# Attention operands split in three parts: high parts in two buffers, rests and low parts on GpSimd, another order of loads and stores

## The reference, cut to what matters

```python
# token stage, for each of the 4 batches
scores = q @ k.T                        # 1024 x 1024
h = prelu((gamma * scores) @ v @ Wo + bo)
# attention stage: 8 heads of 8 features, 4 x 8 = 32 heads in all
xn = layernorm(h)
q, k, v = split(xn @ qkv_w + qkv_b)
h = h + softmax(q * scale @ k.T + bias) @ v @ proj_w + proj_b
# expert stage: layernorm twice, top 2 of 8 experts, weights from a softmax
h = h + sum_e w_e * (gelu(xn2 @ W1[e] + b1[e]) @ W2[e] + b2[e])
```

## Time and profile before

| | us |
|---|---|
| median of 3 runs | 549.04 |
| lowest, highest run | 546.72, 556.23 |
| the profiled execution | 548.42 |
| its span, first to last instruction | 546.5 |
| PE busy | 517.1 (95%) |
| DVE busy | 455.0 (83%) |
| ACT busy | 356.9 (65%) |
| POOL busy | 88.8 (16%) |

### The profile page before, as it was taken

How to read it: one execution, slowest core, us unless ns; L and a number is a source line. 1 busy time by engine, 2 the same in 40 slices (tenths; PEclk the granted TensorE clock), 3 DMA queues, 4 the chain that set the end, 5 groups by cost and what they waited for, 6 DMA issues and landing times.

```text
span 546.5 us, 12886 instructions
## 1 busy us (share of the span) xinstructions
PE 517.1 (95%) x4179; PEld 179.8 (33%) x4179; DVE 455.0 (83%) x538; ACT 356.9 (65%) x633; POOL 88.8 (16%) x186
## 2 busy tenths in 40 slices
PE   7998989698999999999999999999999989999996
PEld 5332333332333333333333333333333343233321
DVE  2679778778999999999999999999999787766644
ACT  2021122245898888898898988988988866455442
POOL 8702021233100100100100001001001360211000
PEclk9999999878999999999999999999999999999999
DMA  7600046983432332332322323323334100100000
GB/s 276 191 4 1 0 129 184 268 241 96 119 88 62 89 83 58 90 78 61 88 76 71 79 75 82 78 65 86 79 85 126 59 11 11 43 20 1 20 19 20
DMA packets 51096, 45.28 MB, mean 83 GB/s; under 512 B 26266, under 2 KB 39035, under 8 KB 51067
## 3 DMA queue, kind: packets, MB, share of 16 engines
q1 hardware_dynamic: 51066, 44.89, 29.6%
HBM read 28.70 MB, written 16.17 MB: 82 GB/s over the span
## 4 chain that ended last, share of the span: by engine, by line
PE 78%; DVE 8%; DMA 5%; issue 3%; SPq 3%; ACT 2%; POOL 1%; DVEq 0%; ACTq 0%; POOLq 0%
PE ps L1516 25%; PE ps L1407 14%; PE ps L1501 12%; PE ps L1677 6%; PE ps L1593 5%; PE ps L1324 3%; PE ps L1335 3%; DVE gated L972 2%; DVE nmax L951 1%; PE ps L1505 1%; PE ps L1421 1%; PE ps L1660 1%; DMA maxima<-max_t 1%; SPq L383 1%; DMA q_ring<-maxima 1%
## 5 line engine op out<-in xcount | busy, mean ns | idle before, releaser
L951 DVE TENSOR_REDUCE nmax<-ps 128x1 f32<-128x1024 f32 x256 | 301.8, 1218 | 19.8 <-PE ps L1407 11.1
L804 ACT ACTIVATE probs<-ps 128x512 f32<-128x512 f32 x512 | 278.1, 596 | 47.3 <-PE ps L1501 37.3
L1516 PE MATMUL ps<-probs,v_ring 128*32 128x256 f32 x2048 | 164.1, 393 | 0.0
L1501 PE MATMUL ps<-q_ring,k_ring 51*128 51x512 bf16 x512 | 100.4, 381 | 5.3 <-ACT probs L804 1.5
L1407 PE MATMUL ps<-k_ring,q_ring 48*128 48x512 bf16 x512 | 100.6, 389 | 2.3 <-DVE nmax L951 1.5
L1516 PEld LDWEIGHTS ps<-probs,v_ring 128*32 128x32 f32 x2048 | 40.5, 108 | 61.9 <-issue 36.9
L1407 PEld LDWEIGHTS ps<-k_ring,q_ring 48*128 48x128 bf16 x512 | 24.7, 93 | 107.5 <-issue 99.2
L1233 DVE TENSOR_TENSOR probs<-probs,ps 128x1024 f32<-128x1024 f32 (+1 forms) x33 | 39.1, 1187 | 25.1 <-PE ps L1660 19.6
L820 ACT ACTIVATE probs<-ps,wide_w 128x1024 f32<-128x1024 f32 x32 | 35.4, 1114 | 33.5 <-PE ps L1593 32.5
L972 DVE SCALAR_TENSOR_TENSOR gated<-ps,v_s,gamma_sb 128x1024 f32<-128x1024 f32 x32 | 40.3, 1278 | 14.9 <-PE ps L1324 13.6
L625 POOL TENSOR_TENSOR max_p<-nmax,zeros 128x8 bf16<-128x8 f32 x32 | 6.5, 202 | 274.7 <-DVE nmax L951 267.0
(11 more groups left out here) (173 smaller groups left out, 348.7 us busy)
## 6 DMA issues: line engine op xcount, KB each, us to landing
k_ring<-qk_parts SPq DMA_DIRECT2D x64, 96.0 KB, 2.4
q_ring<-qk_parts SPq DMA_DIRECT2D x64, 96.0 KB, 2.4
gamma_sb<-gamma_t SPq DMA_DIRECT2D x4, 1024.0 KB, 8.7
v_padded<-v_pad SPq DMA_DIRECT2D x4, 1024.0 KB, 6.1
v_ring<-v_padded SPq DMA_DIRECT2D x32, 128.0 KB, 3.2
outputs<-o_t SPq DMA_DIRECT2D x32, 128.0 KB
qk_parts<-qk_h SPq DMA_DIRECT2D x8, 384.0 KB, 4.7
x_ring<-bias_parts SPq DMA_DIRECT2D x32, 96.0 KB, 3.1
```

The lines of the kernel that those rows point to most:

```text
L804: A.activation(probs[:, s % 4, HALF * j:HALF * (j + 1)], ps[:, key_bank(s, j), :], ACT.Exp).then_inc(exp_done[j], 1)
L951: V.tensor_reduce(nmax[:, par, s:s + 1], ps[:, bank:bank + 2, :].rearrange("p a n -> p (a n)"), AX, ALU.max, negate=True).then_inc(s1_redu ...
L1501: last = mm(ps[:, key_bank(s, j), :], k_ring[rows, u, P * s:P * (s + 1)], q_ring[rows, u, HALF * j:HALF * (j + 1)], start=True, stop=not c ...
L1516: last = mm(ps[VC * j:VC * (j + 1), PVB, 0:2 * P], v_ring[:, u, m, :], probs[:, m % 4, 2 * P * j:2 * P * (j + 1)], start=(m == 0), stop=(m ...
```

## The change

What is computed stays the same; what moves is who splits the operands, and in which order. The steps:

1. `qk_h` has two buffers, used in turn. The high part of batch n waits for the store of batch n - 2 and for the rest of batch n - 2.
2. All rests and low parts are POOL's. DVE's `rest_part` and `low_part` are gone. ACT therefore keeps the float32 value of every batch, those of batches 0 and 1 in `qk_rest`; PE's `project_vv`, which overwrites the PSUM bank, now waits for that copy.
3. DVE's `norm_scale(0)` and `norm_scale(1)` stand behind the first gate of the next batch, where they stood behind the last gate of their own.
4. ACT squares for batches 1 and 2 ahead of the next copy out of PSUM or of the middle part; `square(3)` stands between the high part and the keep of batch 2.
5. POOL's `bias_residual`, which adds the projection's bias to h, stands ahead of `power` for batches 0 to 2.
6. SP loads the operands of heads 0 and 1 behind batch 0's stores, those of head 2 behind batch 1's and those of head 3 behind batch 2's stores of high, values and middle. Batch 1's values are stored between its high and its middle part. At the end, the maxima of head 0 go out ahead of batch 3's high part, and the rows come back ahead of batch 3's values.

The diff, cut to its core:

```diff
-        qk_h = sb("qk_h", [P, T], bf16)
+        qk_h = sb("qk_h", [P, 2, T], bf16)
...
-                sp.wait_ge(qk_h_ready, b + 1)
-                store_parts(b, 0, qk_h)
+                def store_high():
+                    sp.wait_ge(qk_h_ready, b + 1)
+                    store_parts(b, 0, qk_h[:, b % 2, :])
+
                 if b == B - 1:
-                    send_max_rows(0, 0, 0, store_values)
-                elif b >= LATE:
+                    send_max_rows(0, 0, 0, store_high)
+                else:
+                    store_high()
+                if b >= LATE:
+                    store_values()
+                if b == 1:
                     store_values()
                 sp.wait_ge(qk_m_ready, b + 1)
                 store_parts(b, 1, m_of(b))
+                if b == 0:
+                    store_values()
                 if b < LATE:
-                    store_values()
                     store_low(b)
...
-                    for u in range(RING):
+                    for u in range(2):
                         load_operands(u, u)
                         load_values(u, u)
+                elif b < RING - 1:
+                    load_operands(b + 1, b + 1)
+                    load_values(b + 1, b + 1)
...
-            for n in range(B):
+            for n in range(B - 1):
+                if n == B - 2:
+                    rest_part(n - 1)
+                bias_residual(n)
                 power(n)
-                if n < B - 1:
-                    bias_residual(n)
+                if n == B - 3:
+                    rest_part(n - 1)
+                if n >= 1:
+                    low_part(n - 1)
+            power(B - 1)
             rest_part(B - 2)
             split_maxima(0, 0)
             rest_part(B - 1)
...
             def high_part(n):
...
-                act.wait_ge(qk_stored[0], n * 2 * 16)
-                if n == B - 1:
-                    act.wait_ge(qk_r_ready, n)
-                A.activation(qk_h[:, :], flat(5, 7), ACT.Identity, bias=qk_bias[:, 0:1]).then_inc(qk_h_ready, 1)
+                if n >= 2:
+                    act.wait_ge(qk_stored[0], (n - 1) * 2 * 16)
+                    act.wait_ge(qk_r_ready, n - 1)
+                A.activation(qk_h[:, n % 2, :], flat(5, 7), ACT.Identity, bias=qk_bias[:, 0:1]).then_inc(qk_h_ready, 1)
...
                 if b >= 2:
                     leave_hn(b - 2)
+                if b == B - 1:
                     high_part(b - 2)
+                    keep_part(b - 2)
                 if b >= 1:
                     square(b - 1)
+                if b == B - 2:
+                    high_part(b - 2)
+                    keep_part(b - 2)
                 if b >= 2:
                     middle_part(b - 2)
...
-                    if b == B - 1 and s == 0:
-                        low_part(0)
+                    if b >= 2 and s == 0:
+                        norm_scale(b - 2)
...
-                    if b >= 1 and s == NT - 1:
+                    if b == B - 1 and s == NT - 1:
                         norm_scale(b - 1)
...
             def project_vv(n):
 
-                if n < LATE:
-                    pe.wait_ge(qk_r_ready, n + 1)
-                else:
-                    pe.wait_ge(qk_kept, n - LATE + 1)
+                pe.wait_ge(qk_kept, n + 1)
```

More of the change, by code:

```diff
@@ L591, in rest_part @@
             def rest_part(n):
-                pool.wait_ge(qk_kept, n - LATE + 1)
+                pool.wait_ge(qk_kept, n + 1)
                 pool.wait_ge(qk_h_ready, n + 1)
-                gp.tensor_tensor(rest_of(n), rest_of(n), qk_h[:, :], ALU.subtract).then_inc(qk_r_ready, 1)
+                gp.tensor_tensor(rest_of(n), rest_of(n), qk_h[:, n % 2, :], ALU.subtract).then_inc(qk_r_ready, 1)
             def low_part(n):
@@ L598, in low_part @@
                 pool.wait_ge(qk_m_ready, n + 1)
-                pool.wait_ge(qk_l_ready, LATE)
+                if n >= LATE:
+                    pool.wait_ge(qk_l_ready, LATE)
+                pool.wait_ge(qk_stored[2], min(n, LATE - 1) * 2 * 16)
                 gp.tensor_tensor(low_of(n), rest_of(n), m_of(n), ALU.subtract).then_inc(qk_l_ready, 1)
@@ L720, in keep_part @@
             def keep_part(n):
-                act.wait_ge(tok_scored, (n + 1) * NT)
+                if n < LATE:
+                    act.wait_ge(qk_l_ready, n)
+                else:
+                    act.wait_ge(tok_scored, (n + 1) * NT)
                 A.activation(rest_of(n), flat(5, 7), ACT.Identity, bias=qk_bias[:, 0:1]).then_inc(qk_kept, 1)
@@ L775, in _ @@
             high_part(B - 2)
+            square(B - 1)
             keep_part(B - 2)
-            square(B - 1)
             leave_vv(B - 2)
@@ L1010, in first_center @@
                 norm_center(h_all[:, NT * n:NT * (n + 1), :], n)
-            def rest_part(n):
-                dve.wait_ge(qk_h_ready, n + 1)
-                dve.wait_ge(qk_l_ready, n)
-                V.scalar_tensor_tensor(out=qk_rest[:, :], in0=ps[:, 5:7, :].rearrange("p a n -> p (a n)"),
-                                       scalar=qk_bias[:, 0:1], in1=qk_h[:, :], op0=ALU.add,
-                                       op1=ALU.subtract).then_inc(qk_r_ready, 1)
-            def low_part(n):
-                dve.wait_ge(qk_r_ready, n + 1)
-                dve.wait_ge(qk_m_ready, n + 1)
-                dve.wait_ge(qk_stored[2], n * 2 * 16)
-                V.tensor_tensor(qk_l[:, :], qk_rest[:, :], qk_m[:, :], ALU.subtract).then_inc(qk_l_ready, 1)
             leave_v(0)
@@ L1045, in _ @@
                             leave_v(b + 1)
-                    if b == B - 1 and s == 5:
-                        rest_part(1)
                     if b >= 1 and s == 5:
@@ L1051, in _ @@
                         norm_var(b - 1)
-                    if b == B - 2 and s == NT - 1:
-                        rest_part(0)
                     if b == B - 1 and s == NT - 1:
                         row_max(0, 0, 0)
-                        low_part(1)
-                    if b >= 1 and s == NT - 1:
+                    if b == B - 1 and s == NT - 1:
                         norm_scale(b - 1)
@@ L1493, in _ @@
                 keep_busy(3 if i < 2 * NT - 2 else 0)
-            pe.wait_ge(qk_kept, B - LATE)
+            pe.wait_ge(qk_kept, B)
             pe.wait_ge(v_pad_ready, B)
```

## The result

The changed kernel takes 542.8 us, the kernel before 549.41 in the same comparison (medians of 20 runs each): ratio 0.9884, 95% interval 0.9858 to 0.991. The changed kernel is 1.2% faster, some 6.4 us, clear of the measurement's own uncertainty, and within 2%. Forecast were 540 and 1.6%, with 535.5 to 545 as the range.

A forecast was written before the change was run, and what follows sets the result against it. Before the attention loop, PE, DVE and POOL wait for each other, so the loop's start counts: leads of 1.5, 4.5, 4.9 and 8.0 us, cumulative, reach 8.3; 548.42 - 8.3 = 540.1, forecast 540, range 535.5 to 545.

The forecast's parts named there:

- the late maxima: Rival: stores hold head 0's rows of maxima; loop start at 120 to 122, time 542.5 to 544.5 us; chance 0.22.
- two signs of being wrong: Wrong if the loop start's lead is other than 6 to 11 us, or if the lead differs at the end.
- Part 1: Batch 1 to 2: with the gate ahead of hn, PE reaches its next continuous stretch 1.5 us earlier.
- Part 2: Batch 2 to 3: rests and low parts off DVE; project_vv(1) 4.5 us earlier, 1.5 of it from Part 1.
- Part 3: GpSimd's four new instructions hold up DVE's xc and hn of batch 2 by 1.1 and 1.4; lead 4.9 us at turn_hn(2).
- The rival that it would cost 8.5 us: Each of four meetings of GpSimd and DVE costs a whole 2.12 more, in series; time 550.7 us; chance 0.06.
- Part 4: Batch 2 to the last norm: two buffers and a shorter queue bring turn_hn(3) 8.0 us earlier.
- Part 5: Head 0's maxima through DRAM: SP's earlier sends done at 110.6, hidden by 0.5 us; rows back at 117.6.
- the sum: The attention loop starts at 117.6 instead of 125.9, 8.3 us less; 540.1 for the profiled execution.
- the bound of 120: Upper bound for the loop's start, if the high part's 768 KB hold the rows of maxima 2.5 us longer.
- the lead stays: Behind the loop's start the order is the same on all engines, so the 8.3 us last to the end.
- the one that had the clock stay up: No clock fall: 1.4 us less before the transposition, at most 1.4 in head 0; chance 0.27, shared with a missed meeting.

The follow-up runs named there:

- a_dve: The changed kernel with rests and low parts of batches 0 and 1 back on DVE; ratio 0.9875 to the kernel before.
- b_norm: The kernel before with hn of batches 0 and 1 behind the next batch's first gate and the additions to h_all ahead of power; ratio 0.9942.
- b_sq: The kernel before with ACT's square of batch 1 ahead of the high part of batch 0; ratio 0.9961.
- b_two: The kernel before with two buffers for the high part and nothing else; ratio 0.9998.
- b_loads: The kernel before with only the operand loads moved: heads 0 and 1 behind batch 0's stores, 2 behind batch 1's, 3 behind batch 2's; ratio 0.9991.
- a_rows: The changed kernel with head 0's rows of maxima ahead of the stores of batch 3's high part; ratio 0.9948 to the kernel before.
- a_best_end: The changed kernel with rows first, batch 3's values later, 3 fillers, and 2 each ahead of the expert stage's first turned norm and logits; ratio 0.9844.
- a_best_dve: The changed kernel with rows first, batch 3's values later, 3 fillers, and batches 0 and 1's rests and low parts on DVE; 544.34 us, ratio 0.9889.

## Why the prediction was right, and where it was off

The time, 542.8, lies in the stated range, but not in the forecast's own band (538.5 to 542, chance 0.45); it lies in that of the late maxima (542 to 545, 0.22). Of the two signs of being wrong that the prediction names, the first did not come: the start leads by 6.9 us, or 7.4 without the correction for the gate. The second did: the lead is not the same at the end, 3.9 in the profiles. So the right total is in part the width of the range. The losses below are those of one pair of profiles; how the 6.4 us between the medians divide is not shown.

*Part 1* was 1.5 us, measured 1.7. Its cause is not quite as told: of the 1.75 us of `hn`, 1.1 were spent in a meeting with GpSimd's addition to h_all, which the prediction did not see, and which the change moves too.

*Part 2* has its sum right (4.5 against 4.7) and its reason wrong. The 4.5 comes from laying PE's work end to end, which holds whatever frees PE. But I let it come from DVE's freed path, rests and low parts included. a_dve puts them back and loses 0.26; b_norm and b_sq have 2.8 and 2.1 without touching them. What freed PE were the gate ahead of `hn` (with the addition ahead of `power`) and the square ahead of the high part. Once these had moved, PE was the bound, and DVE had room for the rest and the low part.

*Part 3*, the price of the meetings, was 1.1 + 1.4, and the lead at `turn_hn(2)` 4.9; it is 4.7. One meeting was not with `xc` but with the instruction ahead of it: `nmean`, 8 elements per partition, held from 84.33 to 85.91 by the rest that ran until 85.89. `xc` ended at 86.64, or 87.2 counted as in the profile before, forecast 86.9. The warning of the Trainium skill (Perfetto Trace Analysis, "Optimizing Scalar/DVE Operations") that moving work between GpSimd and DVE might not help is borne out by a_dve: it brought nothing. The rival that it would cost 8.5 us did not come; GpSimd's instructions kept to 2.12 to 2.14.

*Part 4* was right: 8.0 at the last norm, measured 7.7, 8.0 at the transposition, measured 7.8. b_two and b_loads each show 2.9 of it, of 3.1 forecast; that both are there was one more than needed.

*Part 5* and the sum are the terms that were mis-sized. SP was not free at 110.6 but, on the same clock of the first gate, 2.2 later: the middle part's stores took 2.5 to issue instead of 1.3, and head 3's six loads 3.9 instead of 2.8. The way out was 1.1 shorter than said and the way back 0.7 longer; with them the start came 1.5 later than said, inside the bound of 120 that stood beside it. a_rows gives 1.4 of that back and starts at 117.7 counted as in the profile before, so PE's queue was at the time forecast. Then "the lead stays" failed: head 0 took 1.3 us longer than before, at a clock that was low for longer. The last 1.7 of the profile lie in the expert stage. The rival that had the maxima late was thus partly true, and the one that had the clock stay up came the other way round in head 0. At the last norm a_dve shows it: with the clock up the transposition came 1.7 earlier (94.56 against 96.24), forecast 1.4.

## What to carry to other kernels

When two engines wait for each other, first change the order of what is there; b_norm and b_sq gave the whole lead at `project_vv(1)` by moving `hn`, the square and an addition to another place on their own engines, while the work moved to GpSimd (four instructions, three of which held DVE up) gave none. Two cures of one wait, a second buffer and an earlier store, do not add. A send that the critical path waits for should not stand behind bulk loads on its queue, and when it is brought forward, look at the next such send: the delay moved on from head 0 to head 1.

## What the runs showed of the hardware

The tail behind the fourth transposition is the same work on PE in the same order in all kernels but a_best_end, and it took from 395.9 us to b_two's 404.7 in the profiles (b_loads apart). Most of the difference is the granted clock around 440 to 460 us, behind two waits of PE of 0.6 us: the six profiles in which it did not fall there have 395.9 to 397.2, the five in which it fell briefly 397.2 to 398.1, and b_two and a_best_dve, in which it stayed low for long, 404.7 and 404.4. PE's rows of the kernel before, then of b_two:

```profile
442.99 0.66 PE L1546 MATMUL ps<-ident,hn 128*128 128x128 f32 x4 [0.63 <-DVE hn L941]
...
459.16 1.13 PE L1593 MATMUL ps<-gamma_sb,up_w 64*128 64x512 f32 x4 [0.52 <-DVE gamma_sb L1195]
```

```profile
439.36 0.65 PE L1546 MATMUL ps<-ident,hn 128*128 128x128 f32 x4 [0.63 <-DVE hn L941]
...
464.05 1.13 PE L1593 MATMUL ps<-gamma_sb,up_w 64*128 64x512 f32 x4 [0.52 <-DVE gamma_sb L1195]
```

The same work took 16.2 us before and 24.7 in b_two, behind the same wait of 0.63. b_two's stretch from 445 to 450:

```profile
445.00:450.00 5.00, 5.00 (x29) 2.17 (x28) 2.86 (x9) 2.46 (x5) 1.64 (x1) 0.50 0.09 28
```

An edit that moves the loop by two or three microseconds can thus be covered by something 300 us later, larger than itself, and a comparison of this kernel needs the profile's times up to the loop beside its medians.

A DVE instruction over 8 elements (0.17 us) stood 1.4 us longer for a GpSimd instruction; the Trainium skill (SBUF — State Buffer, section "Who interferes with whom") names this kind of operation (`tensor_scalar`) among those that can take the port pair that DVE shares with GpSimd, and the 1.58 agrees.
